# A decoder layer on one core: scores in plain fp32, one 32-partition strip per head

## The reference, cut to what matters

```
q, k, v of attention 1 come from x by products of the low-rank weights (rank 64)
x = LN(x + attention1(x))                         # causal, 256 keys
q = x Wq;  k, v = [ctx, x] Wkv                    # 512 context keys, then 256 own keys, causal
x = LN(x + softmax(q k^T / sqrt(8)) v Wout + bout)
s = x Win + bin                                   # 64 features
h = relu(s[..., None] * W1 + b1)                  # 64 x 16 hidden
g = sum_h(h * W2) + b2
x = LN(x + g Wout + bout)
```

## Time and profile before

| | us |
|---|---|
| median of 3 runs | 309.76 |
| lowest and highest | 308.98, 311.21 |
| profiled execution, span from first to last instruction | 309.5 |
| PE busy | 277.4 (90%) |
| VectorE busy | 234.5 (76%) |
| ScalarE busy | 174.3 (56%) |
| GpSimd busy | 72.6 (23%) |

### The profile page before, as it was taken

How to read it: one execution, slowest core, us unless ns; L and a number is a source line. 1 busy time by engine, 2 the same in 40 slices (tenths; PEclk the granted TensorE clock), 3 DMA queues, 4 the chain that set the end, 5 groups by cost and what they waited for, 6 DMA issues and landing times.

```text
span 309.5 us, 6148 instructions
## 1 busy us (share of the span) xinstructions
PE 277.4 (90%) x2240; PEld 181.3 (59%) x2240; DVE 234.5 (76%) x540; ACT 174.3 (56%) x365; POOL 72.6 (23%) x108
## 2 busy tenths in 40 slices
PE   4918678899999999999999999999999999999762
PEld 3706566576776657665656565665665666554431
DVE  2797716587775998888889878799778799777463
ACT  1520235456556567756667566776676658667430
POOL 8996601001202020301111211013101112112211
PEclk9985969999999999999999999999999999999795
DMA  6669999302034512120006200033000000000001
GB/s 188 243 190 303 258 300 229 137 3 55 4 124 85 175 35 102 54 103 3 1 2 162 48 1 2 1 86 71 2 3 2 2 2 1 3 2 17 2 18 34
DMA packets 16109, 23.64 MB, mean 76 GB/s; under 512 B 1648, under 2 KB 11824, under 8 KB 15952
## 3 DMA queue, kind: packets, MB, share of 16 engines
q1 hardware_dynamic: 13632, 14.19, 16.4%
q0 software_dynamic: 2160, 7.47, 8.0%
q10 hardware_dynamic: 288, 1.59, 1.4%
HBM read 13.02 MB, written 9.96 MB: 74 GB/s over the span
## 4 chain that ended last, share of the span: by engine, by line
PE 72%; DVE 17%; DMA 3%; issue 3%; SPq 1%; ACT 1%; POOL 0%; POOLq 0%; ACTq 0%; DVEq 0%
PE psum L1122 15%; PE psum L1104 13%; PE psum L1067 9%; PE psum L1075 7%; DVE pmax L869 5%; PE psum L1077 4%; PE psum L1130 4%; PE psum L1106 4%; DVE w2x L821 3%; DMA qm<-shift_rows 3%; PE psum L1084 3%; PE psum L1108 2%; DVE nmax_s L880 2%; DVE nmax_s L881 2%; PE psum L1159 1%
## 5 line engine op out<-in xcount | busy, mean ns | idle before, releaser
L735 ACT ACTIVATE probs<-psum 128x512 f32<-128x512 f32 x224 | 127.1, 594 | 61.0 <-PE psum L1104 36.1
L869 DVE TENSOR_REDUCE pmax<-psum 128x1 f32<-128x512 f32 (+2 forms) x176 | 111.9, 682 | 19.6 <-PE psum L1067 10.4
L1104 PE MATMUL psum<-qm,ks 98*128 98x512 f32 x176 | 79.9, 463 | 0.0
L1122 PE MATMUL psum<-probs,v 128*9 128x256 f32 (+1 forms) x1024 | 60.6, 354 | 0.0
L1075 PE MATMUL psum<-ks,qm 96*128 96x128 f32 (+1 forms) x256 | 51.0, 309 | 8.2 <-DVE probs L810 8.2
L1067 PE MATMUL psum<-ks,qm 96*128 96x512 f32 x128 | 52.6, 424 | 0.0
L1075 PEld LDWEIGHTS psum<-ks,qm 96*128 96x128 f32 x256 | 43.1, 202 | 13.1 <-issue 9.6
L866 DVE TENSOR_REDUCE nmax<-psum 128x2 f32<-128x512 f32 (+1 forms) x48 | 31.8, 687 | 18.4 <-PE psum L1077 18.3
L1104 PEld LDWEIGHTS psum<-qm,ks 98*128 98x128 f32 x176 | 33.1, 191 | 17.5 <-ACT probs L735 13.3
L669 POOL TENSOR_SCALAR_AFFINE_SELECT probs<-probs 128x512 f32<-128x512 f32 x32 | 19.7, 634 | 96.5 <-ACT probs L735 96.5
L1122 PEld LDWEIGHTS psum<-probs,v 128*9 128x9 f32 x1024 | 21.7, 90 | 31.2 <-issue 9.4
(11 more groups left out here) (133 smaller groups left out, 291.4 us busy)
## 6 DMA issues: line engine op xcount, KB each, us to landing
qm<-scr_q SPq DMA_DIRECT2D x28, 96.0 KB
ks<-scr_k SPq DMA_DIRECT2D x6, 384.0 KB, 4.4
ks<-scr_m POOLq DMA_DIRECT2D x2, 768.0 KB, 7.6
ks<-scr_m SPq DMA_DIRECT2D x2, 768.0 KB, 6.4
ctxT_sb<-ctxT ACTq DMA_DIRECT2D x1, 1024.0 KB, 8.2
scr_m<-probs POOLq DMA_DIRECT2D x2, 512.0 KB, 7.1
qm<-shift_rows SPq DMA_DIRECT2D x64, 4.0 KB
scr_k<-split_k SPq DMA_DIRECT2D x4, 256.0 KB, 2.0
```

Source lines behind the costliest of these rows:

```text
L735: nc.scalar.activation(probs[:, ring % PRING, h:h + nh, q0:T], src, ACT.Exp, scale=SCALE).then_inc(exp_done, 1)
L869: nc.vector.tensor_reduce(pmax[:, t % 2, col:col + nh, part], tile, axis=AX.X, op=ALU.max).then_inc(max_done, 1)
L1104: nc.tensor.matmul(tbank[n % TBANKS], keys, queries, start=True, stop=True).then_inc(scoresT_ready, 1)
L1122: last = nc.tensor.matmul(obank[t % OBANKS][32 * j:32 * j + HS + 1, q0:T], v, probs[:, pv_no[s] % PRING, j, q0:T], start=(kt == 0), stop=( ...
```

## The change

The scores are computed by plain fp32 matmuls. Head j of a group has its 8 channels in partitions 32j to 32j+7 of one tile that holds queries and keys side by side (`qk0` for unit 0, `qk` for the rest, `km` for the context keys), and the negated maximum in partition 32j+8 (a row of ones on the keys' side). The score matmuls take 8 rows for the maximum (L846, L852) and 9 for the exponential (L875). The splits, the stacking and the zeroed tiles are gone; copies to scratch and back remain, once and in one format. Unit 0 is made in the strip layout directly by PE from padded weights (`stacked`), without scratch. Each score bank now belongs to one head; attention 1 has one bank of 384 columns (128 + 256) per head, and so have the own keys of attention 2, where 512-column context banks stay. The exponential's banks hold pairs of key tiles of one head. Seven banks rotate through all purposes and one holds the heads. `norm` is done once per unit. The MLP's first two layers become one product with 1024 columns of scaled weights (`win1`), and its last two another (`wout2`); both are plain fp32 (`hid`, `mo`). The planner is new, with other costs.

```diff
-STACK = HG * SLOTS * HS
-ROWS = STACK + 2
+STRIP = 32
+DATA = HS
+ROWS = DATA + 1
+WIDE = HG * STRIP
...
+BANKS = 7
+PRING = 4
...
+def s_banks(t):
+
+    own = [("own", j, 0) for j in range(HG)]
+    return own if kind(t) == 1 else [("mem", j, qt) for qt in range(QT) for j in range(HG)] + own
+
+
+def pairs(t):
+
+    return [(0, 1)] if kind(t) == 1 else [(0, 1), (4, 5), (2, 3)]
...
+        def strip(tile, j, rows):
+            return tile[STRIP * j:STRIP * j + rows]
...
+            for r in range(DATA, ROWS):
+                dst = qk[r:P:STRIP, :, :, T:].rearrange("p b g t -> p (b g) t")
+                sp.dma_start(dst, ones_t[:, 0:T].unsqueeze(1).to_broadcast([HG, B * NG, T])).then_inc(ones_k, 16)
...
+                    for qt in range(QT):
+                        dst = qk_of(u)[DATA:P:STRIP, g, qt * P:(qt + 1) * P]
+                        sp.dma_start(dst, shift_rows[qt:HG * QT:QT, t % ROWBUFS, :]).then_inc(rows_in[g], 16)
...
-                        link(nc.vector.tensor_copy(high.bitcast(F32R), whole))
-                        nc.vector.tensor_sub(low, whole, high).then_inc(nmax_ready, 1)
...
+            def first(g, start_bank):
+                m = bank(start_bank)
+                nc.tensor.matmul(m[:, 0:T], wq_s[:, g * WIDE:(g + 1) * WIDE], xT_sb[:, 0:T], start=True, stop=True)
+                nc.tensor.matmul(m[:, T:], wk_s[:, g * WIDE:(g + 1) * WIDE], xT_sb[:, 0:T], start=False, stop=False,
+                                 skip_group_check=True)
+                nc.tensor.matmul(m[:, T:], ones_rows[:, :], ones_in[:, :], start=False, stop=True,
+                                 skip_group_check=True).then_inc(first_ready, 1)
...
+                    if src == "mem":
+                        nc.tensor.matmul(m, strip(tile, j, DATA)[:, g, qt * P:(qt + 1) * P], strip(km[:, b], j, DATA)[:, g, :],
+                                         start=True, stop=True).then_inc(s_ready, 1)
+                    else:
+                        at = 0
+                        for q in range(QT):
+                            keys = (q + 1) * P
+                            nc.tensor.matmul(m[:, at:at + keys], strip(tile, j, DATA)[:, g, q * P:(q + 1) * P],
+                                             strip(tile, j, DATA)[:, g, T:T + keys], start=(q == 0), stop=False,
+                                             skip_group_check=True)
+                            at += keys
+                        blocks = m[:, 0:3 * P].rearrange("p (n k) -> p n k", n=3)[:, 0:3:2, :]
+                        nc.tensor.matmul(blocks, ident_b[:, :], neg[:, :, :], start=False, stop=True,
+                                         skip_group_check=True).then_inc(s_ready, 1)
...
+                    for n, kt in enumerate(pairs(t)[p]):
+                        if diagonal(t, p):
+                            keys = strip(tile, j, ROWS)[:, g, T + n * P:T + (n + 1) * P]
+                            q0 = n * P
+                        else:
+                            keys = strip(km[:, b], j, ROWS)[:, g, kt * P:(kt + 1) * P]
+                            q0 = 0
+                        last = nc.tensor.matmul(m[:, n * T:n * T + T - q0], keys, q[:, q0:], start=(n == 0),
+                                                stop=(n == 1 and kind(t) == 2), skip_group_check=True)
+                    if kind(t) == 1:
+                        blocks = m[:, 0:3 * P].rearrange("p (n q) -> p n q", n=3)[:, 0:3:2, :]
+                        last = nc.tensor.matmul(blocks, ident_b[:, :], negT[:, :, :], start=False, stop=True,
+                                                skip_group_check=True)
...
-                    m = open_misc(s)
-                    nc.tensor.matmul(m[:, 0:T], wbc("in2"), x2T[s[1]], start=True, stop=True).then_inc(misc_ready, 1)
+                    elif what == "hid":
+                        for k in range(2):
+                            f = 2 * i + k
+                            last = nc.tensor.matmul(m[:, k * T:(k + 1) * T], win1[:, f * P:(f + 1) * P], x2T, start=True,
+                                                    stop=True)
+                    elif what == "mo":
+                        for i in range(QT):
+                            for f in range(FG):
+                                last = nc.tensor.matmul(m[:, i * C:(i + 1) * C], hid[:, f, i * P:(i + 1) * P], wout2[:, f, :],
+                                                        start=(f == 0), stop=(f == FG - 1))
```

More of the change, by code:

```diff
@@ L73 @@
[L73 to L94, removed]
@@ L182, in ready, with bank_for, take_bank @@
[L182 to L187, removed]
+        if what in ("ln1", "wo", "mo") and any(x[0] == "apply" for x in chain):
+            return NEVER
+        return when(*follows[what](*s[1:]))
+    def bank_for(start):
+        k = min(range(BANKS), key=lambda i: (max(bank_at[i], start), bank_at[i]))
+        return k, max(bank_at[k], start)
+    def take_bank(s, start):
+        k, _ = bank_for(start)
+        bank_of[s], before_in_bank[s] = k, holder[k]
+        holder[k] = s
+        return k
@@ L188, in emit @@
+    def emit(s, begin=None):
+        plan.append(s)
         what, n = s[0], s[1]
-        r = ready(s) if what not in ("max", "exp", "pv") else start(s)
         if s in chain:
             chain.remove(s)
[L192 to L201, removed]
@@ L214, in emit @@
[L214 to L239, removed]
+        r = ready(s)
@@ L301, in schedule @@
-    lead = 0
+                chain.append(("norm", n // NG))
+        elif what == "rows":
+            done[s] = run("sp", r, 150) + 2300
+            done[("rows_in", n)] = done[s]
+        elif what == "put":
+            done[s] = run("sp", r, 80) + 2300
+            chain.append(("take",) + s[1:])
+        elif what == "take":
+            done[s] = run("sp", r, 300) + 2600
+            done[("q_in" if s[1] == "qk" else "m_in", s[2])] = done[s]
+            spl_taken.append(s)
+        elif what == "ln1":
+            end = run("dve", r + 60, DVE_COST["ln1"])
+            done[s] = run("pool", end + 60, POOL_COST["rstd"]) + 60
+            chain.append(("apply", "ln1", n))
+        elif what == "apply":
+            done[s] = run("dve", r, DVE_COST["apply"]) + 60
+            if s[1] != "mo":
+                run("pool", done[s], POOL_COST["after"])
+                chain.append(("x1T" if s[1] == "ln1" else "x2T", s[2]))
@@ L302, in schedule, with spl_free @@
+    def spl_free():
+        n = len(spl_order) - SPL
+        return [("put",) + spl_order[n]] if n >= 0 else []
+    done[("q_in", 0)] = COST["start"]
+    chain += list(LATE)
+    maxima = [("S", t, i) for t in range(STEPS) for i in range(len(s_banks(t)))]
+    exps = [("T", t, p, j) for t in range(STEPS) for p in range(len(pairs(t))) for j in range(HG)]
+    pvs = [("pv", t, p) for t in range(STEPS) for p in range(len(pairs(t)))]
     while maxima or exps or pvs or chain:
         now = free["pe"]
-        idle = [s for s in chain if s[0] not in MISC and ready(s) <= now + COSTS["slack"]]
+        idle = [s for s in chain if s[0] not in MISC and ready(s) <= now + COST["slack"]]
@@ L306, in schedule @@
         if idle:
-            emit(idle[0])
+            emit(min(idle, key=ready))
             continue
-        best = [(NEVER, 0, 0, None)]
-        for k, s in enumerate(chain):
-            if s[0] == "late":
-                due = COSTS["start"] + COSTS["late_from"] + COSTS["late_gap"] * LATE.index(s[1:])
-                best.append((max(now, ready(s), due), 0, k, s))
-            elif s[0] in MISC:
-                best.append((max(now, ready(s)), MLP_RANKS[s[1]] if s[0] in MLP and s[1] < B - 1 else 0, k, s))
@@ new lines, in _ @@
+                    n = s_no[s]
+                    src, j, qt = s_banks(t)[i]
+                    if n == 0:
+                        dve.wait_ge(pm_ready, 2)
+                    if i == len(s_banks(t)) - 1 and t >= ROWBUFS:
+                        sem_, value = misc_ready(("shift", t - ROWBUFS))
+                        dve.wait_ge(sem_, value)
+                    dve.wait_ge(s_ready, n + 1)
+                    m = bank(bank_of[s])
+                    pm = pm1 if kind(t) == 1 else pm2
@@ new lines, in _, with open_bank @@
+            folded(9, w64c("dkv"), ve[:, :])
+            pe.wait_ge(fold_act, 4)
+            first(1, 5)
+            first(2, 6)
+            pe.wait_ge(first_act, 1)
+            first(3, 4)
+            pe.wait_ge(fold_act, 5)
+            pe.wait_ge(first_act, 2)
+            pe.wait_ge(first_dve, 2)
+            pe.wait_ge(neg_ready, 2)
+            pe.wait_ge(ident_ready, 1)
+            pe.wait_ge(heads_zero, 1)
+            def open_bank(s):
+                before = before_in_bank[s]
+                if before is not None:
+                    sem_, value = emptied(before)
+                    pe.wait_ge(sem_, value)
+                return bank(bank_of[s])
@@ new lines, in _ @@
+                    if p == 0 and t:
+                        pe.wait_ge(drained, t)
```

(11 more changed lines are left out.)

1436 lines of the change are left out of this document (606 added, 830 removed).

## The result

The changed kernel takes 875.79 us (median of 4 runs, 873.48 to 877.65) against 310.49 before (median of 4): 2.82 times as long, 95% interval 2.812 to 2.836. One of the four runs before, 316.29 us, was of a slower kind at a lower clock, and the ratio leaves it out. Some 1.8 us of a run lie around its span (877.65 us for a span of 875.9), not 0.3. The prediction was 500, with a range of 400 to 610. The sign was right, the size was not, and one row of the page says why. The page of the changed kernel: busy us with share and instructions, then tenths in 40 slices, PEclk the granted clock.

The account below looks back on a forecast made before the run. TensorE's streaming was taken to bound the kernel: 138 masked banks, 28 masks, 158 strips, 67 values and 81 rest make 472, plus 16 ahead and 13 behind, about 500 us; range 400 to 610.

Parts of the forecast that it names:

- the sum: Whole kernel: TensorE 472 us from the first score, 16 ahead and 13 behind, 501, said as 500.
- rival E: Score strips with 9 of 128 rows in use drop the clock to 1.2 GHz; 850 us or more, chance 0.05.
- a masked bank: Attention 1 score bank of 384 fp32 columns: 0.645 passes, 0.13 mask, 0.30 mode change, 1.075 us; 128 banks, 138 us.
- the mode: Changing TensorE to strips and back at a mask: 0.30 us, taken from column strips, bounds 0 and 0.30.
- D: Score strips: masks hold only their own strip or later heads pass, so four run side by side; 267 us, chance 0.10.
- B: Row strips: changing mode costs nothing, 296 entries at 0.30 us saved, 89 less; 411 us, chance 0.16.
- C's serial form: Attention 2 strips do not overlap at all: 302 us instead of 158, total 644; chance 0.12.
- The number format: Score matmuls in fp32 strips: 324 us against 131 before for the same work, overlap and mode included.
- The lead-in: Before the first score: unit 0 made in strip layout by PE, scores starting near 16 us (13 to 20).
- A first product: Lead-in, making unit 0: four first products at about 1.1 us each.
- a step of attention 2: Second attention on TensorE: about 18.7 us a step.
- costed at nothing: VectorE (below 235 us) and ScalarE (below 195) idle under PE's 500; row DMAs and GpSimd's mask of probabilities hidden.

Follow-up runs that it names:

- micro1: Separate test kernel, no decoder: 13 TensorE stretches, each of one kind of matmul (128 or 64 rows, strips of 32 or 8, masked banks), behind whole-array bf16 work; 522.63 us.
- stacked_fp32: The kernel before with keys and queries declared plain fp32, its 96 and 98 rows, banks and order kept; 569.59 us, ratio 1.833.
- rows128: The changed kernel with all 128 rows in every fp32 score matmul, so no strips, overlap or mode change at masks; 593.88 us, ratio 1.907.
- nomask: The changed kernel without the bf16 mask matmuls, strips of 8 and 9 rows kept; 627.18 us.
- nomask32: The changed kernel without the bf16 mask matmuls and with 32 rows in each strip, the added ones zeroed; 479.74 us.

## Why the prediction was wrong

- **The step that failed is the clock.** Every duration in the sum was taken at 2.4 GHz, and rival E had 0.05 with "850 or more". It came to pass at 876: the granted clock was 0.50 for 740 us, a masked bank took 1.90 us and not 1.075, and with all 128 rows in the same passes it was 594 us at 1.00. Its evidence was misread: the value matmuls, which kept 1.00 in the earlier trace rows, use few columns but all 128 rows. No row of before had few rows in use, and what the clock does there was an unknown. It should have been bounded at both of its levels, not excused by a row that differs in just that respect.
- **The mechanism under it was right.** A masked bank costs 1.06 us at full clock (1.075 predicted), 0.29 of it for the mode (0.30). Masks let nothing pass (D falls). The mode change is not free (B falls), in line with the Trainium skill's rule in "TensorEngine Tiling (Array Packing)", Key Properties. Strips run side by side: four in micro1, two as seen at 563.21 (C's serial form falls). An estimate from these: if all of the kernel went by the masked bank, it would take 876 x 1.06 / 1.90 = 489 us at full clock, where the sum was 500.
- **The number format** was priced at 193 us more for the scores (324 against 131) including overlap and mode; alone and serial it measured 259 (stacked_fp32), where the same prices gave 278.
- **The lead-in was mis-sized:** 30.1 us to the first score, not 16. A first product took 3.16 us, priced at 1.1, so the four are 8 of the 14 us; a pass of 256 columns takes 0.43 there. My prices mixed the 0.57 of a fold, read in a prologue that ran at half clock too (its eight passes of 256 columns, L1004, took 3.47 us), with passes at full clock.
- **At half clock not all doubles.** A masked bank is 1.90, not 2.12, and a step of attention 2, with the work beside it, about 32 us where twice the prediction is 37. So 876 lies below twice the sum.
- **Where the 565 us went,** by the runs: format 310 to 570; the rest of the redesign at full rows 570 to 594; strips of 8 rows instead of whole ones 594 to 876, in which the gain of overlap and the loss of mode changes are contained and the halved clock outweighs them. The second of these is only roughly the redesign's, since rows128 also does without strips and their overlap. The split of that last 282 into clock, overlap and mode at full clock was not measured in the whole kernel; no run had 8-row strips at full clock.
- VectorE and ScalarE never bound, the DMAs never showed, as costed at nothing.

## What to carry to other kernels

Before a layout is narrowed, ask of each long stretch how much of TensorE's array it will have in use, and price the stretch at both levels of the clock unless a row of the same kind shows which it keeps: here a matmul over 8 rows ran nearly twice as long as one over 128 at the same column count (38.0 us against 20.8 for 24), and filling unused rows with zeros paid (627 to 480 us from nomask to nomask32). It did not pay back the change: no variant with fp32 scores came under 479 us, and the rounded format over all rows took 353 against 310. A matmul over the whole array between strips ended their overlap here and cost 0.29 us for the change of mode; count these first. And what is only a common shift of a softmax row needs no exact value, if all keys of the row get the same one.

## What was not expected of the hardware

- PE was busy 740 of 740 us at a granted clock of 0.50. In micro1 one strip of 32 rows ran at 0.55 and 64 rows at 1.00, with PE 99 and 100% busy.
- After work over the whole array the first strips still ran fast: in micro1 three masked banks took 1.06 us each, the fourth 1.45, and the next 1.90.
- The clock's row can be wrong at the start. The changed kernel's window from 20 to 60 us says 0.90, while banks at 31.97 us already took 1.90. The pace of the passes is the safer witness there, and the mean clocks given for whole kernels are some hundredths too high for it.
- Second passes of fp32 matmuls don't hold up the next strip's first ones: eight passes on two strips took 1.88 us at half clock, hardly more than four passes of 0.43. Nor does a bank's second matmul hold the other strip's first, although the program has it ahead: had it held it, the eight passes would take at least six pass times. The Trainium skill's page "TensorE: Matmul & The Clock Gate", Part 3, has starts strictly in program order; the trace shows otherwise for passes and matmuls on different strips.
